# Ten key pairs' row maxima beside the experts instead of eight, and router logits and values from one matmul

## What is computed

```python
xn = layernorm(x)
# attention branch
zn = layernorm(xn) * ln_w + ln_b
q, k, v = split(zn @ W_qkv + b_qkv)            # 16 heads of 8
s = xn + softmax(q @ k.T / sqrt(8)) @ v @ W_proj + b_proj
# expert branch, from xn and not from zn
logits = xn @ Wr + br                          # 8 experts, best two kept
f = sum_e weight_e * (gelu(xn @ W1[e] + b1[e]) @ W2[e] + b2[e])
return x + s * silu(f)
```

## Time and profile before

| | us |
|---|---|
| median of 3 runs | 1101.2 (1100.84 to 1102.49) |
| profiled execution, its own time | 1103.0 |
| its span in the trace | 1101.2 |
| first up-projection matmul | at 14.2 |
| first exponential of attention | at 513.4 |
| last exponential | at 1086.1 |
| busy: PE, DVE, ACT, POOL | 1029.3, 883.7, 866.9, 368.0 |
| mean granted PE clock | 0.988 |

### The profile page before, as it was taken

How to read it: one execution, slowest core, us unless ns; L and a number is a source line. 1 busy time by engine, 2 the same in 40 slices (tenths; PEclk the granted TensorE clock), 3 DMA queues, 4 the chain that set the end, 5 groups by cost and what they waited for, 6 DMA issues and landing times.

```text
span 1101.2 us, 17451 instructions
## 1 busy us (share of the span) xinstructions
PE 1029.3 (93%) x5865; PEld 444.1 (40%) x5897; DVE 883.7 (80%) x1589; ACT 866.9 (79%) x1190; POOL 368.0 (33%) x555
## 2 busy tenths in 40 slices
PE   4998999999999999999999999999999999999997
PEld 3675666666666666664222222122222121122222
DVE  5647877787878787765999899989998998899943
ACT  6876667676767677666898998989898989798985
POOL 4786656657666667554001000001000001000010
PEclk9999999999999999999999999999999999999998
DMA  6432221414142232324212221212112221122102
GB/s 183 123 99 68 66 83 31 120 30 121 31 107 50 64 80 51 97 51 120 51 44 53 55 53 39 68 40 54 42 52 51 56 53 42 51 53 54 25 24 82
DMA packets 99410, 72.02 MB, mean 65 GB/s; under 512 B 21693, under 2 KB 83834, under 8 KB 99322
## 3 DMA queue, kind: packets, MB, share of 16 engines
q1 hardware_dynamic: 99322, 70.92, 24.5%
HBM read 53.12 MB, written 15.46 MB: 62 GB/s over the span
## 4 chain that ended last, share of the span: by engine, by line
PE 34%; ACT 8%; DVE 7%; issue 2%; SPq 1%; DMA 0%; POOL 0%; ACTq 0%; DVEq 0%; POOLq 0%
PE psum L1055 17%; PE psum L1034 8%; ACT p_ring L869 8%; PE psum L999 7%; DVE neg_max_half L1318 7%; PE psum L1084 1%; ACT o_sb L860 1%; DMA den<-o_sb 0%; SPq L469 0%; PE psum L1098 0%; PE psum L1010 0%; SPq L473 0%; DVE neg_max_rest L1327 0%; DVE y L1379 0%; POOL h_lo L685 0%
## 5 line engine op out<-in xcount | busy, mean ns | idle before, releaser
L869 ACT ACTIVATE p_ring<-psum 128x1024 f32<-128x1024 f32 x512 | 494.8, 1026 | 59.7 <-PE psum L1034 54.3
L1318 DVE TENSOR_REDUCE neg_max_half<-psum 128x1 f32<-128x512 f32 x768 | 481.6, 681 | 44.5 <-PE psum L999 36.7
L1055 PE MATMUL psum<-p_ring,v_sb 128*9 128x512 f32 x2048 | 269.2, 598 | 0.4 <-ACT o_sb L860 0.3
L823 ACT ACTIVATE h_hi<-psum,cols 128x512 fp32r<-128x512 f32 x192 | 132.4, 690 | 132.2 <-PE psum L949 131.2
L999 PE MATMUL psum<-k_max_stack,q_max_stack 48*128 48x512 bf16 x768 | 202.2, 380 | 16.6 <-DVE neg_max_half L1318 16.3
L1336 DVE TENSOR_REDUCE neg_max_half<-psum 128x1 f32<-128x512 f32 x256 | 169.3, 683 | 51.7 <-PE psum L985 45.0
L685 POOL TENSOR_TENSOR h_lo<-h_split,h_hi 128x512 fp32r<-128x512 f32 x128 | 165.1, 1294 | 135.4 <-ACT h_split L826 135.2
L1034 PE MATMUL psum<-q_stack,k_stack 51*128 51x512 bf16 x1024 | 200.0, 386 | 3.4 <-ACT p_ring L869 2.2
L635 POOL CAST neg_max_parts<-neg_max_rest 128x16 bf16<-128x16 f32 x32 | 6.3, 197 | 493.6 <-DVE neg_max_rest L1327 493.5
L1034 PEld LDWEIGHTS psum<-q_stack,k_stack 51*128 51x128 bf16 x1024 | 49.5, 93 | 299.2 <-ACT p_ring L869 276.2
L947 PE MATMUL psum<-xn_t_hi,w_hi 128*128 128x512 f32 x256 | 144.8, 566 | 0.7 <-DVE neg_max_half L1336 0.5
(11 more groups left out here) (129 smaller groups left out, 957.5 us busy)
## 6 DMA issues: line engine op xcount, KB each, us to landing
expert_w_bc<-expert_w_dram SPq DMA_DIRECT2D x64, 256.0 KB, 5.1
k_rows_dram<-qk_parts SPq DMA_DIRECT2D x24, 256.0 KB, 3.1
q_max_stack<-q_rows_dram SPq DMA_DIRECT2D x64, 96.0 KB, 2.5
k_max_stack<-k_rows_dram SPq DMA_DIRECT2D x64, 96.0 KB, 2.5
q_stack<-q_rows_dram SPq DMA_DIRECT2D x64, 96.0 KB, 2.4
k_stack<-k_rows_dram SPq DMA_DIRECT2D x64, 96.0 KB, 2.5
q_rows_dram<-qk_parts SPq DMA_DIRECT2D x8, 384.0 KB, 2.6
xz<-in_L_attn_z_dram SPq DMA_DIRECT2D x8, 256.0 KB, 3.2
```

The lines of the kernel that those rows point to most:

```text
L823: act.activation(hh[:, (g * HS + j) % HR, :], up, ACT.Gelu, bias=col(C_B1 + i))\
L869: act.activation(p_sb[:, n % PR, a, :, :].rearrange("p h t -> p (h t)"), scores_bank[s % 2], ACT.Exp, scale=SCALE).then_inc(S("P"), 1)
L1055: i = pe.matmul(o_bank[at:at + VR, :], v_sb[:, b * KT + kt, 2 * (p % PB) + hh, :], p_sb[:, n % PR, a, hh, :], start=(kt == 0), stop=(kt == ...
L1318: dve.tensor_reduce(mx[:, p % MXR, c, hh * NT + t:hh * NT + t + 1], ring_bank(("max", u)), AX.X, ALU.max, negate=True).then_inc(S("R"), 1)
```

## The change

1. `EARLY_PAIRS` goes from 8 to 10: 320 products and reduces in the same 216 slots of the expert phase (27 slots for 40 instead of 32), and 704 in attention, from block 2 to block 239. `EARLY_TURN` and the places of `sp_max_rows` are written anew: pairs 2, 5 and 8 are loaded ahead of the next x in groups 2, 4 and 6.
2. Router logits and values come from one matmul a token tile: the stationary operand is the transposed xn, the moving one [W_v * ln_w | W_r] of 136 columns. The second norm's factor is applied to the result by DVE, one `scalar_tensor_tensor` for each of the four tiles, in slot 14 instead of slot 28. At the start ACT scales the value weights by ln_w, the PE multiplies ln_b with them, and DVE adds that to the bias. `v` (slot 25) and `logits` are gone.
3. Each constant at the start has a semaphore of its own, the value bias is loaded two weights earlier.
4. q, k and what follows of a group stand one slot later; clearing the output bank moves from the start of attention into the last group.

```diff
-        EARLY_PAIRS = 8
+        EARLY_PAIRS = 10
+        MAX_FROM = 2
...
-            upto = [min(len(SINGLES), -(-((n + a) * len(SINGLES)) // MAX_BLOCKS)) for a in range(2)]
+            upto = [min(len(SINGLES), -(-max(0, n + a - MAX_FROM) * len(SINGLES) // (MAX_BLOCKS - MAX_FROM)))
+                    for a in range(2)]
...
-        EARLY_AT = [HT + 4 + (27 * m) // 32 for m in range(EARLY)]
+        EARLY_AT = [HT + 4 + (27 * m) // 40 for m in range(EARLY)]
...
-        EARLY_TURN = [2 * HT + 2, 2 * HT + 28, 3 * HT + 26, 4 * HT + 26, 5 * HT + 26, 6 * HT + 26, 7 * HT + 5, 8 * HT + 1]
+        EARLY_TURN = [g * HT + at for g, at in ((1, 28), (2, 26), (3, 26), (3, 30), (4, 26), (5, 26), (5, 30), (6, 26),
+                                                (7, 9), (7, 30))]
...
-                if g in (2, 3):
-                    sp_max_rows(sp, g)
+                for p in {2: [2], 4: [5], 6: [8]}.get(g, []):
+                    sp_max_rows(sp, p)
                 if g + 1 < NG:
                     sp_load_x(sp, g + 1)
                 spread_w(g)
-                if g > 2:
-                    sp_max_rows(sp, g + 1)
...
+                for p in {2: [3], 3: [4], 4: [6], 5: [7], 6: [9]}.get(g, []):
+                    sp_max_rows(sp, p)
...
-                return {4: [newton(g, 1)], 10: [newton(g, 2)], 21: [rest(0)], 22: [rest(1)],
-                        25: [third(0)], 26: [third(1)]}
+                return {4: [newton(g, 1)], 10: [newton(g, 2)], 22: [rest(0)], 23: [rest(1)],
+                        26: [third(0)], 27: [third(1)]}
...
+                def value_weights():
+                    act.wait_ge(S("lnb_v"), 1)
+                    act.activation(wvr_sb[:, 0:D], wvr_sb[:, 0:D], ACT.Copy, scale=col(C_LNW))\
+                        .then_inc(S("wv"), 1)
...
+                def logits_and_values():
                     wait(pe, "xh", g, 1, 1)
+                    wait(pe, "kf", g, 1, 0)
                     if g == 0:
-                        pe.wait_ge(S("const"), 4 * 16)
+                        pe.wait_ge(S("wr"), 16)
+                        pe.wait_ge(S("wv"), 1)
                     for t in range(TT):
-                        m = pe.matmul(b5[:, t * E:(t + 1) * E], xnT[:, t * P:(t + 1) * P], wr_sb[:, :],
-                                      start=True, stop=True)
-                    m.then_inc(S("lg"), 1)
+                        m = pe.matmul(lv[:, t, :], xnT[:, t * P:(t + 1) * P], wvr_sb, start=True, stop=True)
+                    m.then_inc(S("lv"), 1)
...
-                return {9: [t1], 12: [logits], 15: [t2], 18: [qk], 21: [w_t], 25: [v]}
+                return {8: [value_bias] if g == 0 else [], 9: [t1], 12: [logits_and_values], 16: [t2], 19: [qk], 22: [w_t]}
...
+                    for t in range(TT):
+                        i = dve.scalar_tensor_tensor(
+                            v_sb[:, g * TT + t, :, 0:DH], lv[:, t, 0:D].rearrange("p (h d) -> p h d", h=H),
+                            nwt[:, 4, t:t + 1], bv_bc[:, :].rearrange("p (h d) -> p h d", h=H), ALU.mult, ALU.add)
+                    i.then_inc(S("vd"), 1)
...
-                        7: [guess_rsqrt(g, 2)], 12: [low_x], 15: [router_top],
+                        7: [guess_rsqrt(g, 2)], 11: [value_bias] if g == 0 else [], 12: [low_x], 14: [router_top, values],
                         17: [router_weights], 18: [router_sum], 19: [router_done],
-                        24: [second(0)], 25: [second(1)], 28: [values]}
+                        25: [second(0)], 26: [second(1)]}
```

66 lines of the change are left out of this document (37 added, 29 removed).

## The result

| | before | after |
|---|---|---|
| median, us | 1101.2 (1100.84 to 1102.87, 15 runs) | 1105.15 (1102.21 to 1112.46, 15 runs) |
| span of the profiled execution | 1101.2 | 1107.4 |

A forecast was written before the change was run, and what follows sets the result against it. No single engine was taken as the bound; attention's block lengths decide. Terms -36.5 +14.7 +1.2 -7.6 +10.5 +1.5 gave -16.2 us, from 1101.2 to 1085.0 us, range 1073 to 1097 (8 in 10).

The forecast's parts named there:

- -7.6: Router logits and values in one matmul: the logits' 0.95 us of PE time is saved eight times, -7.6 us.
- The new wait of the second transpose for the values ... costs nothing: Expert phase, slot 16 behind slot 14: free while reduces for PE's products in slots 15 and 16 follow the values.
- the bulge at slot 14: Expert phase: a fourth place per group where DVE's delay reaches PE, 0.45 us each, part of the +10.5.
- DVE in the expert phase ... I take +10.5: Added reduces and values fit DVE's 46.7 us idle on average, not at bulges: four places x 0.45 x 6 groups.
- DVE absorbs: Rival: DVE's 46.7 us idle time covers the early reduces, so the +10.5 is 0; 1074.5 us, chance 0.17.
- idle time before reduces under 20 us: Expert phase, sign that the forecast is right: DVE's idle time before reduces falls from 46.7 to under 20 us.
- Four such are 1.12.: DVE's values as four instructions of 128 columns, 0.28 us each: 1.12 us, +0.44 a group over one of 0.68.
- Attention, -36.5: 240 blocks summed by kind (four products, transpose, copy, plain): -35.1 us, plus -1.4 for the wait ahead of block 3.
- The last early transpose: Expert phase: each of two more transposes of maxima was priced at 0.6 us, +1.2 together.
- x late, +1.5: Expert phase: next x stands behind the later q and k stores, so DVE waits longer, +1.5 us (bounds 0 and 3).
- Constants, 0: Start of the kernel: the first up-projection's inputs come no earlier, 0 us (bounds -1 and +1).
- PE bounds attention: Rival: in attention a product taken away returns only its 0.23 us, 14.7 instead of 36.5; 1106.8 us, chance 0.09.

The follow-up runs named there:

- e1: The kernel before with ten early pairs and the change's places of products, loads and transposes, old matmuls kept; 1102.08 us, ratio 1.0004.
- e5: The changed kernel with eight early pairs at their old places, values of tile 0 in slot 14 and the other three in slot 16; 1102.67 us.
- e2: The changed kernel with eight early pairs, placed and loaded as before; 1113.82 us, ratio 1.0107.
- e13: The changed kernel with values split over slots 14 and 16, last early transpose at slot 257, DVE's `h_lo` one slot later; 1090.27 us.
- e10: The kernel before with ten early pairs, last early transpose at slot 257 and DVE's `h_lo` one slot later; 1085.46 us, ratio 0.9848.
- e4: The kernel before with DVE's `h_lo` subtraction one slot later in its list; 1096.87 us, ratio 0.9954.
- e14: e10 with attention's products starting at block 0 instead of block 2; 1082.24 us, ratio 0.9831.
- e6: e1 with the last early transpose at slot 257 instead of 254; 1099.96 us, ratio 0.9987.
- e3: The changed kernel with DVE's `h_lo` subtraction one slot later in its list; 1098.32 us, ratio 0.9971.

## Why the prediction was wrong, step by step

Of the 20 us between 1085.0 and 1105.15, the ten pairs alone account for about 9 (forecast -8.6, measured 0 in e1), and the joint matmul beside them for 10.7 (forecast -7.6, measured +3.1).

- **"The new wait of the second transpose for the values ... costs nothing"**, and 0.45 us for the bulge at slot 14. This step failed, and with it the **"-7.6"** of the logits. Beside ten pairs the part costs 3.1 us where it was to give 7.6; beside eight it costs 11.6, of which e5 takes 11 back. The transpose does wait for the values, 2.17 us in group 0, where no reduce comes between. I looked at the order of values and reduces in DVE's list, and not at what stands ahead of the values: two operations of 32 columns, stretched to 2.2 us beside POOL's work in e2 and to 1.5 to 2.0 in groups 1 to 6 of e13, though the earlier trace rows showed the same stretch elsewhere. The 1.0 us a group saved on PE is real (slot 24) and is lost again in slots 14 to 20.
- **"DVE in the expert phase ... I take +10.5"**, argued from DVE's idle time before reduces. The number was near right for ten pairs alone (27.9 forecast for their whole cost, 28.6 measured in e1), and that is luck, for the reason was not right. I took the bulges for load. Nearly half of DVE's idle time in that stretch stood before another instruction, `h_lo` (40.9 us before, beside 46.7 before reduces), and so was not to be had. With that wait out of the way the added reduces cost next to nothing (e10 against e4: 17.6, by e14's trace 14.1, with 15.9 forecast for PE alone). So "DVE absorbs" was right on what DVE's load allows, and the order of its list stood against it. The sign that I gave for the forecast, idle time before reduces under 20 us, did not come (40.1).
- **"Four such are 1.12."** Right: 1.11 us for the four. The Trainium skill (VectorE: DVE Perf Modes, the TRN2 errata) gives an estimate of 1.03 by its figures; the trace is 0.08 above it.
- **Attention, -36.5.** The kinds held, the arithmetic around them did not. The kinds' sum fell from 533.1 to 500.9, 32.2 us; my -35.1 was made against the measured 536.0, which already held the 1.7 us wait at the start, and then I took 1.4 for that wait once more. And I counted no block as late in the changed kernel, where six are, by 1.7 and 1.6 us at the start (the clock) and some 5 together at the reciprocals. Less what the other blocks are below the forecast's lengths (plain ones 1.96 for 2.00) that is 5.5: 500.9 + 5.5 = 506.4, so -29.6.
- **The last early transpose**, slot 254 of 256, was priced at 0.6 like the others. It has nothing behind which its chain can hide: 3.4 us more in slot 29, of which 2.1 come out (e6).
- **x late, +1.5**: DVE's wait for x in the expert phase went from 7.6 to 9.6 us. **Constants, 0**: the first up-projection came 0.6 earlier.
- The rival on the slower side, "PE bounds attention", gave 1106.8, near the time measured, by a mechanism that did not occur: the fourth product of a block was worth its 0.7 us. By its time alone it would look right.
- The Trainium skill (Perfetto Trace Analysis, section "Identifying the Most-Contended Engine") takes an engine's occupancy as a fair measure of nearness to its limit for VectorE, and tells to optimise the fullest engine first. Here DVE was at 78% and set the pace of PE through the order of its list; e3 gains 6.8 us by order alone. The same page's section "Optimization Strategy" has the gaps of an engine followed to the semaphore that ends them, which is what the rows of waits above do.

## What to carry to other kernels

Read an engine's idle time by the instruction that it stands before. Only what stands before the kind of work that you add can be counted as room for it; idle time before another instruction is a wait at the head of an in-order list, and everything behind it is late by as much. Where PE depends on short answers from an engine through two buffers, look first for the instruction in that list that waits for a third engine, and put it later: here this alone was worth 5 us, and made 64 more products cheap (1085.5 and 1082.2 for 1101.2, the best versions). Price a moved step with all that stands ahead of it in the same slot, at the durations that they have there, beside what the other engines do at that moment. And test two parts together as well as alone: here one cost 11.6 us by itself and 3.1 beside the other.

## What the runs showed of the hardware

- Operations of DVE with two inputs in SBUF are stretched beside POOL's `h_lo`, which reads SBUF: the router's subtraction and comparison of 32 columns took 0.84 and 1.32 us in e2_values_only and ended with POOL's instruction, and the comparison takes 0.18 where POOL is through (e10, group 4). The addition of 32 columns with one input in PSUM took 0.17 beside the same instruction in e13 (at 307.88). Reduces, which read PSUM, kept 683 ns. The Trainium skill (SBUF — State Buffer, section "Who interferes with whom") says that a DVE instruction with two SBUF inputs contends with a GpSimd instruction that reads SBUF; the trace agrees.
- The granted clock of PE falls to 0.50 for some microseconds just after attention has begun, before and after the change and in e10 and e14 (0.63 and 0.57 in windows of 4 us). PE had waited in the first blocks. Blocks 2 and 3 are late by 1.9 us before, 3.2 after and 1.4 in e10.
- It falls in the expert phase too, behind waits of PE: after 2.17 us in group 0 of the changed kernel, after 1.99 in group 4 of e2, and in groups 1 and 6 of e10 but not of e14. A matmul of 512 columns then starts every 0.43 us instead of every 0.23.
- Gains do not add: ten pairs (with the late transpose) are worth 2 us, `h_lo` later 5, and both 16.
